# Layer norms on ScalarE, routing arithmetic on GpSimd, masked scores in PSUM and paired steps in a decoder-block kernel

## The chip, the cores and the metric

The kernel runs on one core of one Trainium2 chip. The metric is device time in microseconds, the median of several runs. The engines of a core have queues of their own, each worked off in order: TensorE (PE; its weight loads are shown as PEld), VectorE (DVE), ScalarE (ACT), GpSimd (POOL) and SyncE (SP), which here only issues DMAs. They wait for one another through semaphores.

## The reference

The input x has 4 x 1024 rows of 256 numbers, all float32. Three blocks follow one another, each added to x:

```python
x = x + attention(layernorm(x))       # 16 heads of 64, 4 key/value heads, no causal mask
x = x + cross(layernorm(x), context)  # 16 heads of 16, context of 64 rows, masked softmax
x = x + ffn(layernorm(x))             # routing, then a layer norm with gamma and beta
```

The ffn routes each row: scores against 8 cluster signatures go through a sigmoid and a table of 8 knots with linear interpolation (a calibration); the first largest picks a cluster. The scores of its 8 tiles go through the same calibration, and one tile is picked. A small network (gelu, tanh) gives two numbers per row; the picked tile's spline weights (two products, add, relu, dot product) turn them into one magnitude, which scales the picked tile's direction of 256 numbers. Direction plus input is normalised, times gamma, plus beta.

## The kernel before, in words

The 4096 rows are eight chunks of 512. Self-attention runs in 64 units (a chunk and a pair of heads) of 8 steps, one step for each 128 keys, 512 steps in all. In each step TensorE forms scores for a step (`scores`, L936), multiplies the exponentials of two steps ago with v (`attend`, L956) and forms the scores for a row maximum some steps ahead (`max_d` or `max_s`, L904). ScalarE takes the exponential (L1190) or, in every other step, a relu of the maximum scores too (L1174); VectorE reduces them to row maxima in the steps between (L1433) and adds up the first head's exponentials (L1449); GpSimd adds up the second head's (L1794). The maximum scores have a single pair of PSUM banks, `max_scores`, and so have the key scores.

Everything behind self-attention, for one chunk, is a `tail`: output projection (`out_proj`, `x1`), norm 1, cross-attention (`q2`, eight `scores2`/`soft2`/`exp2`/`weights2T`, `projected2`, `x2`), norm 2, `route`, `compress`, `gelu`, `comp`, two calibrations (`cal_a`, `cal_exp`, `cal_b`, `cal_c`) with `first_max`, `pick_tiles` and `pick_one`, `gathered`, `spline`, `y`, norm 3 with `gamma` and `beta`, `x3` and the store. The tail of a chunk is spread over the 64 attention steps of the next; the last chunk's is done at the end as two halves of 256 rows (`last_tail`), in alternation.

The order of all engines is one list that a planner, `Plan`, writes. A tail is a generator that stops at `yield EARLY` or `yield LATE`. In each step `attention` lets generators go on twice: the early pieces come ahead of TensorE's `attend`, the late ones behind it and ahead of the step's `scores` and maximum. So each `yield` moves what follows to the next such point, and every engine has a step's late pieces in its queue ahead of the step's exponential and row maximum. Pieces of TensorE take banks in turn from a ring of two, `misc` (2 and 6); units take them too (a projection of q, a transpose of maxima, the sums). `ALONE` is an early point at which no unit takes one. `BANK_FREE` names the signal that frees a bank, and how many counts before its end.

A norm is done so: VectorE takes `bn_stats` and `bn_aggr` (L1322, L1325), GpSimd adds epsilon and takes the power -0.5 (L1754, L1757), VectorE subtracts the mean and multiplies (`normalise`, L1329). Cross-attention's `soft2` adds the mask from PSUM into `weights` (L1545), takes the row maximum (L1549) and subtracts it (L1551). The other lines in the rows below: transposes of normed rows (L859), of picked tiles (L1091), the subtraction, products and sums of the knot arithmetic (L1615, L1627, L1630, L1632, L1634), `first_max` (L1641 and following), evictions of ScalarE with a bias (L1229) and without (L1251).

Of the kernel before, what the change touches and what calls it, by code (L numbers as in the profile page):

```python
# [13 lines left out]
P = 128  # L14
# [73 lines left out]
def unit(u):  # L88
# [9 lines left out]
    "x_stats": {"bn_stats": NT, "moments": NT, "var_eps": 1, "rstd": 1}, "x_norm": {"normed": NT},  # L98
# [15 lines left out]
    "out_proj": {"out_proj": 1}, "residual_bias": {"residual_bias": 1}, "x1": {"x1": 1},  # L114
    "stats": {"bn_stats": NT_TIMES, "moments": NT_TIMES, "var_eps": 1, "rstd": 1}, "norm": {"normed": NT_TIMES},
# [5 lines left out]
    "route": {"route": 1}, "route_ev": {"route_done": 1}, "compress": {"compressed": 1}, "gelu": {"gelu": 1},  # L121
    "comp": {"comp": 1}, "tanh_a": {"tanh": 2}, "tanh_exp": {"tanh_exp": 1}, "tanh_b": {"tanh": 3},
    "cal_a": {"gate": 1}, "cal_exp": {"gate_exp": 1}, "cal_b": {"gate": 6}, "cal_c": {"gate": 7},
    "first_max": {"pick": 5}, "pick_tiles": {"pick": 2}, "pick_one": {"pick": 1},
    "pickT": {"pickT": 1}, "pickT_ev": {"pickT_done": 1}, "gathered": {"gathered": 1},
    "gathered_ev": {"small": 1, "directions": 1}, "spline": {"spline": 8}, "y": {"y": NT_TIMES},
    "gamma": {"gamma": NT_TIMES}, "beta": {"beta": NT_TIMES}, "x3": {"x3": 1},
# [31 lines left out]
class Plan:  # L159
# [3 lines left out]
    def __init__(self):  # L163
        self.entries, self.seen = [], set()
        self.total, self.counts = {}, {}
        self.rings = {"max": [0], "key": [3], "misc": [2, 6]}
        self.turn = {name: -1 for name in self.rings}
        self.holder, self.banks = {}, {}

    def put(self, stage, *key):  # L170
# [3 lines left out]
        self.entries.append(entry)  # L174
        for name, times in signals_of(stage, key).items():
# [101 lines left out]
def calibration(plan, j, which):  # L277
# [6 lines left out]
    plan.put("cal_c", j, which)  # L284


def tail(plan, j):
# [3 lines left out]
    for i in range(nt):  # L291
# [5 lines left out]
        yield EARLY if i < nt - 1 else LATE  # L297
    plan.put("stats", j, 1)
    yield LATE
    plan.put("norm", j, 1)  # L300
    yield EARLY
    for c in range(KC):
        plan.put_in_bank("norm_T", j, 1, c)
        yield LATE
# [3 lines left out]
        yield EARLY  # L308
# [43 lines left out]
    for c in range(KC):  # L352
        plan.put_in_bank("norm_T", j, 2, c)
        yield LATE
        plan.put("norm_ev", j, 2, c)
        yield EARLY
    plan.put_in_bank("route", j)
    yield LATE
    plan.put("route_ev", j)
    yield EARLY  # L360
    plan.put_in_bank("compress", j)
    yield LATE
# [11 lines left out]
    plan.put("first_max", j, 0)  # L374
    plan.put("pick_tiles", j)
    yield LATE
    yield from calibration(plan, j, 1)
    plan.put("first_max", j, 1)
# [7 lines left out]
    for i in range(nt):  # L386
        plan.put_in_bank("gathered", j, i)
        yield LATE
        plan.put("gathered_ev", j, i)
        yield EARLY if i < nt - 1 else LATE  # L390
# [6 lines left out]
    yield LATE  # L397
    plan.put("beta", j)
    for pair in range(nt // 2):
        plan.put("x3", j, pair)  # L400
        if pair < nt // 2 - 1:
            yield LATE
# [141 lines left out]
class Workspace:  # L544


    def __init__(self, nt, first, allocate):
# [24 lines left out]
        self.hidden = flat[:, 3 * words:3 * words + 2 * nt * GRID].rearrange("p (a i n) -> p a i n", a=2, i=nt)  # L572
        self.mag = new("mag", nt)
# [3 lines left out]
        self.rstd = new("rstd", 2, nt)  # L577
# [15 lines left out]
def build(nc, ins, out):  # L593
# [5 lines left out]
    with ExitStack() as ctx:  # L599
# [13 lines left out]
        def before(signal, stage, *key):  # L613
            return plan.counts[(signal, stage, *key)][0]

# [141 lines left out]
        def rows_of(j):  # L757
            start = chunk_of(j) * CH + spaces[j].first * P
            return slice(start, start + tiles_of(j) * P)

# [87 lines left out]
        def _(tensor):  # L848
# [237 lines left out]
            def pickT(j):  # L1086
                ps = bank("pickT", j)
                pe.wait_ge(*freed("pickT", j))
                pe.wait_ge(*after("pick", "pick_one", j))
# [27 lines left out]
        def _(scalar):  # L1117
# [5 lines left out]
            def soft(k):  # L1123
                return main.c[:, :, :].rearrange("p a b -> p (a b)")[:, k * (HD + 1):(k + 1) * (HD + 1)]

# [85 lines left out]
            def norm_ev(j, k, c):  # L1211
# [5 lines left out]
                elif j < FIRST_HALF:  # L1217
                    act.wait_ge(*after("spline", "spline", j - 1))
# [4 lines left out]
            def q2_ev(j, m):  # L1223
# [3 lines left out]
                if 1 <= j < FIRST_HALF:  # L1227
                    act.wait_ge(*after("y", "y", j - 1))
# [25 lines left out]
            def route_ev(j):  # L1254
                nt, n = tiles_of(j), CL + TILES
                act.wait_ge(*after("route", "route", j))
                if 1 <= j < FIRST_HALF:
                    act.wait_ge(*after("pick", "pick_one", j - 1))
# [28 lines left out]
            def gathered_ev(j, i):  # L1287
                ps = bank("gathered", j, i)
                act.wait_ge(*after("gathered", "gathered", j, i))
                if 1 <= j < FIRST_HALF:  # L1290
                    act.wait_ge(*after("spline", "spline", j - 1))
# [615 lines left out]
```

## Time and profile before

| | us |
|---|---|
| median of 3 runs | 2048.97 (2048.21 to 2051.25) |
| the profiled execution's own time | 2041.75 |
| its span, first to last instruction | 2040.0 |
| TensorE busy | 1840.0 (90%) |
| VectorE busy | 1265.0 (62%) |
| ScalarE busy | 1135.5 (56%) |
| GpSimd busy | 912.8 (45%) |
| DMA queue 1, share of 16 engines | 5.4% |

The mean granted TensorE clock is 0.954 of full speed. A busy share says how long an engine worked, not whether the end depended on it; the waits and the timeline say that.

### The profile page before, as it was taken

Reading aid. Unit: us, or ns where it says so; the run is one execution under the profiler, and the core shown is the slowest. Engines: PE = TensorE matmul, PEld = TensorE weight load, DVE = VectorE, ACT = ScalarE, POOL = GpSimd, SP = SyncE. Lnnn points to the kernel's source line nnn. Section 1 sums busy time; section 2 is a strip of 40 time slices with the busy share of each in tenths; the row PEclk is TensorE's granted clock in tenths of the full one; section 3 lists DMA queues with packets and bytes.
Section 4 is the critical chain, followed back from the end, with each engine's and each line's share of the span. In section 5 each row is a group of like instructions: output and inputs, shape, how many; then the busy total and the mean of one; then the engine's idle time right before and its main releaser. Section 6 shows DMA issues by size and latency. Waiting matters only on the chain.

```text
span 2040.0 us, 27516 instructions
## 1 busy us (share of the span) xinstructions
PE 1840.0 (90%) x9556; PEld 904.5 (44%) x9556; DVE 1265.0 (62%) x2925; ACT 1135.5 (56%) x1507; POOL 912.8 (45%) x763
## 2 busy tenths in 40 slices
PE   2799999998999889998999989999899989999873
PEld 1554453453644444454454435345364434444341
DVE  4355646658476674756658665666747666475656
ACT  1266755765466654755557564565546655476422
POOL 2055445543554434552635433563454435354521
PEclk8799999998999999998999989999899999999986
DMA  5010000000200000010200000000010000000000
GB/s 151 1 45 19 1 1 1 11 22 1 62 11 1 0 1 21 1 32 1 61 3 11 1 1 21 1 11 21 2 51 1 1 1 22 1 1 1 21 1 10
DMA packets 22874, 32.01 MB, mean 16 GB/s; under 512 B 2576, under 2 KB 16976, under 8 KB 22736
## 3 DMA queue, kind: packets, MB, share of 16 engines
q1 hardware_dynamic: 22736, 30.26, 5.4%
q8 instruction: 75, 1.23, 0.3%
q14 instruction: 63, 0.52, 0.1%
HBM read 13.48 MB, written 4.19 MB: 9 GB/s over the span
## 4 chain that ended last, share of the span: by engine, by line
PE 73%; DVE 16%; issue 4%; ACT 4%; POOL 2%; DMA 1%; SPq 0%; POOLq 0%; DVEq 0%; ACTq 0%
PE attended L956 20%; PE key_scores L936 18%; PE misc L854 7%; PE max_scores L904 5%; PE misc L996 5%; PE misc L1020 3%; DVE relu L1433 2%; PE misc L966 2%; DVE running_sum L1449 2%; PE misc L922 2%; PE misc L1041 1%; PE misc L1052 1%; PE misc L1011 1%; PE misc L859 1%; ACT relu L1174 1%
## 5 line engine op out<-in xcount | busy, mean ns | idle before, releaser
L1190 ACT ACTIVATE probs<-key_scores 128x1024 f32<-128x1024 f32 x512 | 524.6, 1025 | 587.6 <-PE key_scores L936 435.6
L1794 POOL TENSOR_TENSOR prob_sum<-prob_sum,probs 128x512 f32<-128x512 f32 x384 | 507.1, 1321 | 247.7 <-ACT probs L1190 227.1
L956 PE MATMUL attended<-probs,v_all 128*64 128x512 f32 x2048 | 573.9, 634 | 0.7 <-ACT probs L1190 0.7
L1433 DVE CUSTOM_DVE_ANT_0 relu<-max_scores,relu 128x512 f32<-128x512 f32 x512 | 332.4, 686 | 310.1 <-PE max_scores L904 309.5
L936 PE MATMUL key_scores<-q_high,k_chain 64*128 64x512 f32 x2048 | 466.4, 451 | 9.5 <-ACT probs L1190 8.8
L936 PEld LDWEIGHTS key_scores<-q_high,k_chain 64*128 64x128 f32 x2048 | 195.6, 187 | 464.2 <-issue 250.9
L1174 ACT ACTIVATE relu<-max_scores 128x1024 f32<-128x1024 f32 x256 | 261.4, 1021 | 45.5 <-PE max_scores L904 45.5
L904 PE MATMUL max_scores<-k_max,q_high 64*128 64x512 f32 x1024 | 214.3, 414 | 67.9 <-DVE row_max L1433 66.3
L1790 POOL TENSOR_TENSOR prob_sum<-probs 128x512 f32<-128x512 f32 x64 | 86.7, 1354 | 360.9 <-PE misc L966 303.6
L1449 DVE TENSOR_TENSOR running_sum<-running_sum,probs 128x512 f32<-128x512 f32 x320 | 221.6, 692 | 16.1 <-ACT probs L1190 5.4
L936 PE MATMUL key_scores<-q_low,k_chain 64*128 64x512 f32 x1024 | 205.9, 398 | 0.0
L956 PEld LDWEIGHTS attended<-probs,v_all 128*64 128x64 f32 x2048 | 108.1, 137 | 184.8 <-issue 181.4
L1422 DVE SCALAR_TENSOR_TENSOR q_low<-misc,columns_sb,q_high 128x512 fp32r<-128x512 f32 x64 | 48.0, 750 | 170.1 <-ACT q_high L1165 169.7
L904 PEld LDWEIGHTS max_scores<-k_max,q_high 64*128 64x128 f32 x1024 | 99.5, 190 | 113.5 <-DVE row_max L1433 79.3
L1832 POOL TENSOR_TENSOR weights<-weights,row_stat 128x512 f32<-128x512 f32 x56 | 58.4, 1042 | 158.3 <-DVE row_stat L1561 152.9
L854 PE MATMUL misc<-xT,wq_hl 128*128 128x512 f32 x384 | 108.2, 418 | 0.0
L996 PE MATMUL misc<-wo,heads_out 128*128 128x256 f32 x448 | 103.5, 384 | 0.0
L1754 POOL TENSOR_SCALAR rstd<-moments 128x4 f32<-128x4 f32 x29 | 6.9, 238 | 210.3 <-DVE moments L1325 210.3
L936 PEld LDWEIGHTS key_scores<-q_low,k_chain 64*128 64x128 f32 x1024 | 99.4, 191 | 0.0
L996 PEld LDWEIGHTS misc<-wo,heads_out 128*128 128x128 f32 x448 | 82.8, 190 | 17.8 <-issue 7.3
L1803 POOL TENSOR_TENSOR heads_out<-raw_out,inv_sum 128x512 f32<-128x512 f32 x64 | 84.6, 1322 | 7.5 <-ACT inv_sum L1203 2.6
L854 PEld LDWEIGHTS misc<-xT,wq_hl 128*128 128x128 f32 x384 | 68.6, 191 | 34.7 <-issue 22.2
(420 smaller groups left out, 2198.9 us busy)
## 6 DMA issues: line engine op xcount, KB each, us to landing
k_chain<-k_chain SPq DMA_DIRECT2D x32, 256.0 KB, 3.8
buf_a<-in_x SPq DMA_DIRECT2D x8, 512.0 KB, 4.8
k_max<-k_max SPq DMA_DIRECT2D x16, 256.0 KB, 3.7
x_in<-in_x SPq DMA_DIRECT2D x7, 512.0 KB, 4.0
out_x<-buf_b SPq DMA_DIRECT2D x7, 512.0 KB, 3.2
heads_out<-in_qkv_wT SPq DMA_DIRECT2D x1, 1536.0 KB, 8.3
wo<-in_o_wT SPq DMA_DIRECT2D x1, 1024.0 KB, 13.0
rows_sb<-in_rows SPq DMA_DIRECT2D x1, 646.0 KB, 10.7
```

What stands on the lines that cost most here:

```text
L854: done = tensor.matmul(ps_out, lhs(a, c), rhs(b, c), start=n == 0, stop=n == len(terms) - 1)
L904: tensor.matmul(max_scores[:, head, :], q_high[u % 3][rows, i * P:(i + 1) * P], k_max[rows, place, g // 2, first:first + 512], start=True, ...
L936: done = tensor.matmul(key_scores[:, head, :], k_chain[rows, place, part, half, keys], q[rows, :], start=kt == 0 and part == 0 and q is hi ...
L956: tensor.matmul(attended[head * HD:(head + 1) * HD, :], v_all[:, kt, g * HD:(g + 1) * HD], prob_slot(u, kt, head), start=kt == 0, stop=kt ...
L996: done = tensor.matmul(ps[:, 0:D], heads_out[:, p, rows], wo[:, p, :], start=p == 0, stop=p == PAIRS - 1)
L1174: scalar.activation(relu[:, :, :], max_scores[:, :, :], ACT.Relu).then_inc(S["relu"])
L1190: scalar.activation(probs[(u * KT + kt) % len(probs)][:, :, :], key_scores[:, :, :], ACT.Exp).then_inc(S["exp"])
L1433: vector.tensor_tensor_reduce(out=relu[:, head, :], in0=max_scores[:, head, :], in1=relu[:, head, :], scale=1.0, scalar=-3.4e38, op0=ALU.a ...
L1449: vector.tensor_tensor(total, so_far, probabilities, ALU.add).then_inc(S["prob_sum0"])
L1790: gpsimd.tensor_tensor(prob_sum[1][:, :], prob_slot(u, 0, 1), probabilities, ALU.add).then_inc(S["prob_sum1"])
L1794: gpsimd.tensor_tensor(prob_sum[1][:, :], prob_sum[1][:, :], probabilities, ALU.add).then_inc(S["prob_sum1"])
L1803: gpsimd.tensor_tensor(heads_out[:, p, :], raw_out[:, :], inv_sum[:, :], ALU.mult).then_inc(S["heads_out"])
```

## The change

1. `normalise` moves from VectorE to ScalarE: an Identity activation with the reciprocal root as scale and minus mean times root as bias; GpSimd makes this bias with two more operations (`rstd` has four rows instead of two). The third norm is a norm of this kind too; then `gamma` is one product per pair of tiles on VectorE, `beta` is added to the residual rows on GpSimd at norm 2's place in the order, and `x3` adds both, pair by pair.
2. `bn_stats` follows each `x1`, `x2` and `y`; `stats` only aggregates. `y` goes by pairs.
3. `soft2` writes the masked scores back into their PSUM bank, takes the maximum there and subtracts from there into `weights`; the bank is free after that (`behind` 0 instead of 2).
4. `cal_c` is split. VectorE keeps `cal_b` (four operations), `cal_d` (a sum) and `cal_g` (two sums); GpSimd gets `cal_e` (four) and `cal_h` (two), `pick_tiles`, `pick_one` and the first four operations of `spline`; `mag` is the rest of the spline. Each has a step of its own.
5. In `tail`, a step without work follows the first norm too, both `norm_T` share a step, so do `route` and `compress`, and `gathered` goes by pairs.

```diff
-    "stats": {"bn_stats": NT_TIMES, "moments": NT_TIMES, "var_eps": 1, "rstd": 1}, "norm": {"normed": NT_TIMES},
+    "stats": {"moments": NT_TIMES, "var_eps": 2, "rstd": 2}, "norm": {"normed": NT_TIMES},
...
-    "norm_T": ("normT", "norm_ev", 0), "q2": ("q2_done", "q2_ev", 0), "scores2": ("soft2", "soft2", 2),
+    "norm_T": ("normT", "norm_ev", 0), "q2": ("q2_done", "q2_ev", 0), "scores2": ("soft2", "soft2", 0),
...
     plan.put("cal_b", j, which)
     yield LATE
-    plan.put("cal_c", j, which)
+    plan.put("cal_d", j, which)
+    plan.put("cal_e", j, which)
+    yield LATE
+    plan.put("cal_g", j, which)
+    plan.put("cal_h", j, which)
+    yield LATE
+    plan.put("first_max", j, which)
...
     plan.put("norm", j, 1)
+    yield LATE
     yield EARLY
     for c in range(KC):
         plan.put_in_bank("norm_T", j, 1, c)
-        yield LATE
+    yield LATE
+    for c in range(KC):
...
     plan.put_in_bank("route", j)
+    plan.put_in_bank("compress", j)
     yield LATE
     plan.put("route_ev", j)
-    yield EARLY
-    plan.put_in_bank("compress", j)
-    yield LATE
     plan.put("gelu", j)
...
-    for i in range(nt):
-        plan.put_in_bank("gathered", j, i)
+    for pair in range(nt // 2):
+        for i in range(2 * pair, 2 * pair + 2):
+            plan.put_in_bank("gathered", j, i)
         yield LATE
...
     plan.put("spline", j)
-    plan.put("y", j)
-    yield LATE
+    yield LATE
+    plan.put("mag", j)
+    for pair in range(nt // 2):
+        plan.put("y", j, pair)
+        yield LATE
     plan.put("stats", j, 3)
     yield LATE
-    plan.put("gamma", j)
-    yield LATE
-    plan.put("beta", j)
+    plan.put("norm", j, 3)
     for pair in range(nt // 2):
+        yield LATE
+        plan.put("gamma", j, pair)
         plan.put("x3", j, pair)
...
+            def normalise(space, src, dst):
+                for i in range(space.nt):
+                    scalar.activation(dst[:, i, :], src[:, i, :], ACT.Identity, bias=space.rstd[:, 3, i:i + 1],
+                                      scale=space.rstd[:, 1, i:i + 1]).then_inc(S["normed"])
...
+                scores3 = bank("scores2", j, n)[:, :].rearrange("p (h k) -> p h k", h=HB)
...
+                vector.tensor_tensor(scores3, scores3,
+                                     mask_add[:, b * SC:(b + 1) * SC].unsqueeze(1).broadcast_to([P, HB, SC]),
+                                     ALU.add).then_inc(S["soft2"])
+                dve.wait_ge(S["soft2"], base + 1)
+                vector.tensor_reduce(row_stat[:, 0, :], scores3, AX.X, ALU.max).then_inc(S["soft2"])
...
+            def cal_e(j, which):
+                space, n, base = spaces[j], tiles_of(j) * CL, before("knot", "cal_e", j, which)
+                gate, intervals = space.gate, space.intervals
+                pool.wait_ge(*after("gate", "cal_d", j, which))
+                gpsimd.tensor_tensor(intervals[:, :, 0:KNOTS - 1], intervals[:, :, 0:KNOTS - 1], intervals[:, :, 1:KNOTS],
+                                     ALU.subtract).then_inc(S["knot"])
...
```

## Rows read from the trace of the kernel before

**Rows 1.** The page, part 1: busy us and share of each engine.
```profile
PE 1840.0 (90%) x9556; PEld 904.5 (44%) x9556; DVE 1265.0 (62%) x2925; ACT 1135.5 (56%) x1507; POOL 912.8 (45%) x763
```

**Rows 2.** By stretch: us, PE, PEld, DVE, ACT, POOL busy; granted clock, DMA, GB/s.
```profile
0.00:100.00 100.00, 50.17 (x205) 34.11 (x206) 41.71 (x117) 21.15 (x29) 15.29 (x25) 0.76 0.26 77
...
100.00:1925.00 1825.00, 1725.82 (x9085) 833.07 (x9083) 1156.90 (x2607) 1084.09 (x1416) 866.21 (x705) 0.97 0.05 12
...
1925.00:2040.00 115.00, 64.05 (x270) 37.32 (x268) 66.35 (x202) 30.26 (x62) 31.32 (x34) 0.79 0.04 14
...
2000.00:2024.00 24.00, 7.61 (x24) 4.12 (x24) 20.16 (x97) 6.48 (x17) 0.00 (x0) 0.55 0.00 0
```

**Rows 3.** TensorE's waits, 100 to 1925 us: waiter <- awaited: us, times, longest.
```profile
PE max_scores L904 <- DVE row_max L1433: 57.2, 17, 7.1
...
PE misc L859 <- DVE buf_b L1329: 19.8, 6, 4.1
...
PE key_scores L936 <- ACT probs L1190: 8.8, 17, 1.5
...
PE misc L1091 <- DVE buf_c L1665: 6.0, 3, 2.9
...
PE misc L1041 <- POOL weights L1832: 4.9, 5, 1.0
```

**Rows 4.** Timeline, 458 to 464 us: start, duration, work [idle before <- awaited].
```profile
458.17 1.26 POOL L1794 TENSOR_TENSOR prob_sum<-prob_sum,probs 128x512 f32<-128x512 f32 x1
...
458.17 1.30 DVE L1634 TENSOR_TENSOR buf_c<-buf_c 128x32 f32<-128x32 f32 x1
...
459.51 0.19 DVE L1641 TENSOR_REDUCE mag<-buf_c 128x4 f32<-128x32 f32 x1
...
463.86 0.80 PE L904 MATMUL max_scores<-k_max,q_high 64*128 64x512 f32 x2 [5.48 <-DVE row_max L1433]
```

**Rows 5.** Timeline, norms at 14 and at 312 us.
```profile
14.41 2.08 DVE L1329 TENSOR_SCALAR buf_a<-buf_a,moments,rstd 128x256 f32<-128x256 f32 x4
...
311.71 4.36 DVE L1329 TENSOR_SCALAR buf_b<-buf_a,moments,rstd 128x256 f32<-128x256 f32 x4
...
316.12 1.12 PE L859 MATMUL misc<-consts_sb,buf_b 128*128 128x128 f32 x4 [4.12 <-DVE buf_b L1329]
```

**Rows 6.** VectorE lines: L1329 min/median/max ns; L1551 busy us, mean ns.
```profile
L1329 DVE TENSOR_SCALAR buf_b<-buf_a,moments,rstd x56: 399/1358/1443, 311.7 to 1855.8; 128x256 f32<-128x256 f32 x56
...
L1551 DVE TENSOR_TENSOR weights<-weights,row_stat 128x512 f32<-128x512 f32 x56 | 53.8, 960 | 1.9
...
L1551 DVE TENSOR_TENSOR probs<-probs,buf_c 128x512 f32<-128x512 f32 x2 | 1.4, 692 | 0.1
```

**Rows 7.** By stretch, 5 us behind two waits of TensorE.
```profile
315.00:320.00 5.00, 3.88 (x14) 1.86 (x16) 1.67 (x3) 0.60 (x1) 4.23 (x4) 0.66 0.02 3
465.00:470.00 5.00, 5.00 (x16) 1.45 (x12) 3.37 (x12) 2.66 (x4) 1.90 (x2) 0.53 0.00 2
```

**Rows 8.** Timeline, the loop's last long wait and one of the last tail's.
```profile
1890.41 0.79 PE L904 MATMUL max_scores<-k_max,q_high 64*128 64x512 f32 x2 [2.61 <-DVE row_max L1433]
...
2023.44 0.61 PE L1091 MATMUL misc<-consts_sb,p2T 128*64 128x128 f32 x2 [7.49 <-DVE p2T L1665]
```

**Rows 9.** Groups by form, GpSimd and VectorE: busy us, mean ns.
```profile
L1777 POOL TENSOR_TENSOR x_in<-x_in 128x384 f32<-128x384 f32 x8 | 8.0, 1005 | 0.6
...
L1775 POOL TENSOR_TENSOR x_in<-x_in 128x128 f32<-128x128 f32 x8 | 3.7, 458 | 0.6
...
L1627 DVE TENSOR_TENSOR buf_c<-buf_c,rows_sb 128x224 f32<-128x224 f32 x14 | 5.5, 392 | 0.5
...
L1757 POOL TENSOR_TENSOR rstd<-rstd,minus_half 128x4 f32<-128x4 f32 x29 | 30.2, 1041 | 2.4
```

**Rows 10.** Groups by form, ScalarE: 128x256 with a bias and without.
```profile
L1229 ACT ACTIVATE x_in<-misc,columns_sb 128x256 f32<-128x256 f32 x1 | 0.5, 464 | 0.0
...
L1251 ACT ACTIVATE buf_d<-misc 128x256 f32<-128x256 f32 x28 | 10.7, 382 | 3.9 <-PE misc L1030 3.9
```

More of the change, by code:

```diff
@@ L296, in tail @@
         plan.put("x1", j, i)
[L297 removed]
+        if i < nt - 1:
+            yield EARLY
     plan.put("stats", j, 1)
@@ new lines, in cal_d, with cal_g @@
+            def cal_d(j, which):
+                dve.wait_ge(*after("gate", "cal_b", j, which))
+                vector.tensor_reduce(gates_flat(j, 1), spaces[j].intervals[:, :, 1:KNOTS], AX.X, ALU.add).then_inc(S["gate"])
+            def cal_g(j, which):
+                dve.wait_ge(*after("knot", "cal_e", j, which))
+                vector.tensor_reduce(gates_flat(j, 1), picked_knots(j), AX.X, ALU.add).then_inc(S["gate"])
+                vector.tensor_reduce(gates_flat(j, 2), spaces[j].steps_by[:, :, 0:KNOTS - 1], AX.X, ALU.add).then_inc(S["gate"])
@@ L1695, in y @@
+            def y(j, pair):
+                space, tiles = spaces[j], range(2 * pair, 2 * pair + 2)
+                dve.wait_ge(*after("mag", "mag", j))
                 dve.wait_ge(*after("directions", "gathered_ev", j, space.nt - 1))
-                for i in range(space.nt):
+                dve.wait_ge(*after("normed", "norm", j, 2))
+                for i in tiles:
                     vector.scalar_tensor_tensor(
@@ L1709, in beta_ @@
-            def beta_(j):
-                space = spaces[j]
-                dve.wait_ge(*after("rstd", "stats", j, 3))
-                dve.wait_ge(*after("gamma", "gamma", j))
-                for i in range(space.nt):
-                    vector.scalar_tensor_tensor(
-                        out=space.b[:, i, :], in0=space.b[:, i, :], scalar=space.rstd[:, 1, i:i + 1], in1=beta[:, :],
-                        op0=ALU.mult, op1=ALU.add).then_inc(S["beta"])
+                dve.wait_ge(*after("y", "y", j, pair))
@@ L1725, in _ @@
-                "spline": spline, "y": y, "gamma": gamma_, "beta": beta_,
+                "cal_b": cal_b, "cal_d": cal_d, "cal_g": cal_g, "first_max": first_max,
+                "tile_scores": tile_scores, "mag": mag_, "y": y, "gamma": gamma_,
             }
@@ new lines, in cal_h, with pick_tiles @@
+            def cal_h(j, which):
+                gate, base = spaces[j].gate, before("knot", "cal_h", j, which)
+                pool.wait_ge(*after("gate", "cal_g", j, which))
+                gpsimd.tensor_tensor(gate[:, 0], gate[:, 0], gate[:, 2], ALU.mult).then_inc(S["knot"])
+                pool.wait_ge(S["knot"], base + 1)
+                gpsimd.tensor_tensor(gate[:, 6 if which else 3], gate[:, 0], gate[:, 1], ALU.add).then_inc(S["knot"])
+            def pick_tiles(j):
+                tiles = spaces[j].route[:, :, CL:].rearrange("p i (c t) -> p i c t", c=CL)
+                pool.wait_ge(*after("pick", "first_max", j, 0))
+                gpsimd.tensor_tensor(spaces[j].picked_by[:, :, :, :], tiles,
+                                     spaces[j].gate[:, 4].unsqueeze(3).broadcast_to([P, tiles_of(j), CL, TPC]),
+                                     ALU.mult).then_inc(S["picked"])
```

275 lines of the change are left out of this document (138 added, 137 removed), and 2 rows, old and new, of the table SIGNALS.

## The prediction

> **What bounds the kernel now.** I read the busy shares first. TensorE is busy 1840.0 of 2040.0 us, VectorE 62%, ScalarE 56%, GpSimd 45% [rows 1]: TensorE sets the end, so a change elsewhere pays only where TensorE stands still or runs at a lower clock. The table by stretch splits the 200 us of idleness: 50 in the first 100 us, 99 in the 1825 us of the attention loop, 51 in the last 115 us [rows 2]. The table of TensorE's waits then says who is late in the loop: 57.2 us in 17 waits for VectorE's row maxima, 19.8 in 6 for the layer norm written by VectorE, 8.8 for the exponentials, 6.0 for the picked tiles, 4.9 for the cross weights [rows 3]. Those five make 96.7 of the 99.
>
> The timeline shows the mechanism twice. At 458.2 VectorE is inside the knot arithmetic of a tail. A 128x32 operation of that piece takes 1.30 us while GpSimd adds into its running sum, against 0.19 for a neighbour; the row maxima stand behind them in VectorE's queue, `max_scores` is not free, and TensorE waits 5.48 us [rows 4]. At 311.7 the four norm instructions take 4.36 us instead of the 1.6 that 0.4 us each, the fastest, would make; the transposes wait 4.12 us [rows 5, 6]. The median of 1.36 us over 56 such instructions shows that this is the rule in the loop.
>
> The idle time is not all of the loss. In the 5 us after the wait at 463.86 the granted clock is 0.53 with TensorE busy all the time, and it is 0.66 after the one at 316.12 [rows 7], where the engine had just stood still for 4 to 5 us; 1.0 and 0.53 mark the two levels of 2.4 and 1.2 GHz. That costs 5 x 0.47 = 2.4 and 5 x 0.34 = 1.7 us more, 2 us on average. The loop has 17 waits of at least 2.4 us, the first at 316.12 and the last at 1890.41 [rows 5, 8]: some 34 us. So norms and routing hold 99 + 34 = 133 us in the loop at most.
>
> **Part 1: routing.** Now `cal_c` (7 operations), `first_max` (5) and `pick_tiles` (2) share a step, 14 dependent operations ahead of one row maximum, and `cal_b` puts 6 there in another. Afterwards a step holds at most five small ones: four in `cal_b`, one in `cal_d`, two in `cal_g`, five in `first_max`; and the two-input ones that GpSimd held up go to GpSimd. `first_max` keeps three of that kind. Five at 0.19 to 0.4 us are 1 to 1.5 us. I let 85% of 57.2 + 6.0 go: **-54**. What is late next is GpSimd: VectorE's `cal_g` waits for `cal_e`, four operations. From 458 ns at 128 columns and 1005 at 384 [rows 9] a line gives 0.66 us at 224 and 0.25 at 32, so `cal_e` is 2.3 us against about 1.4 on VectorE (0.39 each, rows_sb form, [rows 9]). It stands behind one running sum of 1.3 us on GpSimd [rows 4]; a step lasts about 3 us, so it is done mostly when asked for. Fourteen calibrations with two such waits at 0 to 2 us each: 0 to 56 us; I take 0.2 each, near the cover, **+5**. The `spline`, `pick` and `beta` pieces on GpSimd are read a step later and lie beside attention; without that cover they would cost their own 1 us per tail.
>
> **Part 2: norms on ScalarE.** The 19.8 us go, and with them the part of the 8.8 us and of the maxima that the slow norm and gamma passes cause (about 4.5): **-24**. ScalarE has to do the norm in its place, ahead of the next exponential in its queue. A 128x256 activation with a bias takes 0.46 us, without one 0.38 [rows 10]; a second per-partition operand should add the same 0.08, so four are some 1.9 to 2.1 us. The Trainium skill (ScalarE: Activation LUTs, What ACT_TABLE_LOAD costs) says that every such pointer operand adds about 93 ns; the bias row agrees, the scale has no row. TensorE has about 0.3 us of slack behind an exponential, but steps with projections have 1 to 2. 27 norms in the loop (7 tails x 3, 6 input blocks), each 0 to 1.8 us: 0 to 49; I take 0.6, because the free step puts the reciprocal root on GpSimd (1.04 us for the power and two more operations of about 0.25, by the line above) behind it: **+16**. Before that step `norm` is queued one step behind `stats`; if GpSimd is late, ScalarE waits and the exponential and relu behind it, then TensorE. That is inside the upper bound.
>
> **Part 3: the two banks.** Pairs of transposes, `route` with `compress`, and pairs of `gathered` now take both banks of the ring in one step. Where a q projection, a transpose of maxima or the sums take one in the same step, TensorE waits for an eviction by ScalarE (0.38 us and more [rows 10]) that stands behind other work. Counting the steps of all seven tails gives 9 such steps. Each costs between 0 (freed in time) and 3 us; I take 1.2: **+11**. The tail's length stays: in the schedule the calibrations add 4 steps, the end 2, the norms take 3 off and the gathers 2, beside 60 to 64 steps now, of 64 that a block of rows has. A tail that runs over makes the next start late, and only the last would show, by a step of 3 us.
>
> **Part 4: scores in PSUM.** The bank is released after the subtraction, 1.4 us later. In two steps of each tail another user is near: 14 times 0 to 1 us; **+3**. The subtraction reads PSUM and one small operand: now 960 ns on average against 692 where GpSimd rests [rows 6], so 56 x 0.27 = 15 us of VectorE go, all hidden; that only makes the 85% likelier.
>
> **Clock.** Of the 34 us, three or four long waits should stay: **-26**.
>
> **The two ends.** At the start the second norm (2.08 us [rows 5]) leaves VectorE, whose chain leads to the key projection; the first is 0.7 us later through two more GpSimd operations: -1. At the end VectorE is busy 20.16 of 24 us with two serial halves [rows 2]; half of that goes to GpSimd, with handovers, and one wait of 7.49 [rows 8] gets shorter: -4. The norms there have no cover: two per half plus the last, 0.6 us more each, and the final scaling about +1: +4. Together **-1**, between -8 and +8.
>
> **Sum**, against the profiled execution's 2041.75 us: -54 + 5 - 24 + 16 + 11 + 3 - 26 - 1 = -70, so 1972. The median of the runs is 7.2 us above the profiled one, so **1979 us** (-3.4%). A run of this kernel tells about 0.2%, 4 us, from no change.
>
> **Rivals.**
> *A, given back inside the loop* (0.15): the exponentials become the wait. 27 norms at 1.5 us (41) and 9 bank steps at 2.5 (23) plus 14 us of GpSimd waits, and waits above 2.4 us keep half of the clock loss (-17): -54 - 24 + 41 + 23 + 14 + 3 - 17 - 1 = -15: 2034. For it: ScalarE is 56% busy and TensorE already waits 17 times on it [rows 3]; against: these waits are 0.5 us on average, and activations of this length occur in each unit without one.
>
> *B, slower, the port and queue of GpSimd* (0.10): the moved arithmetic is at least 1.7 times as long there, and each of its two-input operations holds VectorE's (1.30 for 0.19 [rows 4]). The row maxima then stand behind VectorE waiting for `cal_e`, `pick_tiles` and `cal_h`. Price: if two of GpSimd's 1.3 us operations and `cal_e` line up (4.9 us, less 1.5 of cover), 28 waits of 3.4 us are 95, and the clock loss stays: -54 + 95 - 24 + 16 + 11 + 3 - 1 = +46: 2095. It decides from 1.8 us per wait on, where the sum passes zero (95 - 46 = 49 us over 28). The Trainium skill (GPSIMD Engine Reference, Engine selection) says elementwise work belongs on VectorE, GpSimd being about half as fast with two inputs. The skill (SBUF, Who interferes with whom) calls the pair of ports an exclusive lock against VectorE operations with two SBUF inputs. The rows agree with the lock. By these rules the move would be a loss, were TensorE not waiting on the queue's order rather than on VectorE's sum.
>
> *C, the steps matter and not the engines* (0.02, no change): waits reappear one step on, under other names: within 4 us.
>
> *Forecast* 0.73. Its own range is 1950 to 2012 (norms 0.2 to 1.3, bank steps 0.5 to 2, 70 to 95% of the waits gone). With A inside, 8 times in 10: **1942 to 2032**. Chances: faster 0.73 + 0.15 = 0.88; same 0.02; slower 0.10.
>
> **What would show it.** TensorE's waits on the row maxima under 12 us in the loop, those on the norm in `buf_b` under 3; a busy TensorE near 1810 with a granted clock of 0.98 or more in the loop; waits on the exponentials up from 8.8 to 15 to 30, at norm steps; a few waits at the second transpose, at `compress` and at the second `gathered`. VectorE's busy time down by about 150, GpSimd's up by 80 to 90, ScalarE's by 45 to 60. The forecast is wrong if waits on `cal_e`'s results stand in front of the row maxima, if the waits on exponentials exceed 40 us, or if the clock stays at 0.97.

## The result, and the profile after

The changed kernel takes 2029.93 us (median of 4 runs, 2027.29 to 2033.37) against 2048.59 for the kernel before beside it: ratio 0.9909, interval 0.9889 to 0.993. That is 0.9% faster where 3.4% was forecast. Single runs differ by some us: the profiled one of before was 7 us under its median, the one of after (2033.37) is 3 over, so the two traces differ by only 8.4 us. The result lies inside the stated range by 2 us, and outside the forecast's own range of 1950 to 2012.

First the busy shares of the changed kernel, as in [rows 1].

```profile
PE 1838.3 (90%) x9556; PEld 909.0 (45%) x9556; DVE 1150.5 (57%) x2619; ACT 1196.9 (59%) x1635; POOL 1007.9 (50%) x1011
```

Then its table by stretch, as in [rows 2].

```profile
0.00:100.00 100.00, 50.57 (x208) 34.47 (x208) 39.27 (x110) 25.48 (x38) 15.96 (x29) 0.78 0.26 78
100.00:1925.00 1825.00, 1733.17 (x9138) 840.69 (x9137) 1062.80 (x2364) 1139.96 (x1530) 956.25 (x907) 0.98 0.05 13
1925.00:2032.00 107.00, 54.57 (x214) 33.80 (x212) 48.44 (x147) 31.45 (x68) 35.73 (x75) 0.70 0.02 5
```

And TensorE's waits between 100 and 1925 us, as in [rows 3].

```profile
PE key_scores L961 <- ACT probs L1236: 37.3, 38, 3.6
PE max_scores L929 <- DVE row_max L1473: 27.9, 19, 4.4
PE misc L947 <- DVE weights L1584: 7.1, 10, 0.7
PE misc L879 <- DVE weights L1584: 3.8, 8, 0.5
PE misc L1125 <- ACT shift_row L1226: 2.9, 3, 1.0
PE misc L884 <- DVE q_low L1462: 2.8, 4, 1.2
PE misc L1066 <- POOL weights L1829: 2.6, 4, 0.6
PE misc L1116 <- POOL buf_c L1866: 2.3, 2, 1.2
PE misc L1066 <- DVE weights L1584: 2.2, 3, 0.9
```

VectorE lost 114.5 us and TensorE stands still almost as long as before: all rows of this view make 89.4 us against 98.4. The row maxima fell from 57.2 to 27.9, the norm's 19.8 are gone, and in their place stand 37.3 us on exponentials and 13.1 on banks that `soft2` (L1584) still reads. From the first to the last `attend` the loop is 13.4 us shorter (1837.07, now 1823.70), it starts 0.7 us earlier, and what follows it is 5.7 us longer.

Most of these 5.7 us lie behind the last matmul (1.4 ahead of it). GpSimd adds the first half's result there and only then begins the second half's spline; VectorE waits for that:

```profile
2018.67 1.26 POOL L1805 TENSOR_TENSOR weights<-weights 128x512 f32<-128x512 f32 x1 [1.99 <-DVE weights L1706]
2020.01 0.24 POOL L1876 TENSOR_TENSOR p2T<-probs 128x32 f32<-128x32 f32 x1
...
2021.25 0.19 DVE L1681 SCALAR_TENSOR_TENSOR p2T<-p2T,probs 128x32 f32<-128x32 f32 x1 [2.72 <-POOL p2T L1882]
```

From its statistics to its last addition the second half then takes 4.8 us (2024.1 to 2028.9) where it took 3.6 (2033.7 to 2037.3): the root's two more operations, the activation and the product stand in series.

Three places show what is late now. ScalarE at the second norm of the tail that runs beside a batch's last chunk, GpSimd's queue ahead of it, and TensorE behind it (timelines):

```profile
407.55 1.01 POOL L1774 TENSOR_TENSOR x_in<-x_in 128x384 f32<-128x384 f32 x1
408.64 0.23 POOL L1746 TENSOR_SCALAR rstd<-moments 128x4 f32<-128x4 f32 x1
...
410.38 0.20 POOL L1754 TENSOR_TENSOR rstd<-rstd 128x4 f32<-128x4 f32 x1
...
410.62 2.08 ACT L1153 ACTIVATE buf_b<-buf_a,rstd 128x256 f32<-128x256 f32 x4 [1.34 <-POOL rstd L1754]
412.60 1.00 ACT L1236 ACTIVATE probs<-key_scores 128x1024 f32<-128x1024 f32 x1
...
413.65 0.50 PE L961 MATMUL key_scores<-q_high,k_chain 64*128 64x512 f32 x2 [3.60 <-ACT probs L1236]
```

The root's four GpSimd operations begin only after the key projection's differences (L1774), ScalarE idles 1.34 us for them, the norm takes 2.08, and the exponential starts at 412.60. The change's free step does not help here: it lies behind the norm, ahead of the transposes, and between statistics and norm there is one step as before. Waits of 3.60 and 3.63 us recur at 892.75 and 1373.02. ScalarE's waits for the root in the same 1825 us:

```profile
ACT buf_b L1153 <- POOL rstd L1754: 11.7, 13, 2.3
ACT x_in L1153 <- POOL rstd L1754: 4.6, 4, 1.7
```

So the root was late at 17 of the 27 norms, by 16.3 us in all.

VectorE in `first_max` (L1662 to L1670), then the row maximum (L1473) and TensorE:

```profile
447.67 0.19 DVE L1662 TENSOR_REDUCE mag<-buf_c 128x4 f32<-128x32 f32 x1 [0.74 <-POOL buf_c L1854]
447.89 1.14 DVE L1664 TENSOR_TENSOR buf_c<-buf_c,mag 128x32 f32<-128x32 f32 x1
449.07 1.31 DVE L1666 TENSOR_TENSOR buf_c<-buf_c,consts_sb 128x32 f32<-128x32 f32 x1
...
452.15 0.79 PE L929 MATMUL max_scores<-k_max,q_high 64*128 64x512 f32 x2 [2.52 <-DVE row_max L1473]
```

VectorE where `mag` (L1688) and both pairs of `y` (L1696, each with two `bn_stats`, L1367) stand between two row maxima:

```profile
732.01 1.33 DVE L1688 TENSOR_SCALAR mag<-mag,rows_sb 128x4 f32<-128x4 f32 x1
733.38 0.88 DVE L1696 SCALAR_TENSOR_TENSOR buf_b<-buf_d,mag,buf_b 128x256 f32<-128x256 f32 x2
734.29 0.75 DVE L1367 BATCH_NORM_STATS2 stats<-buf_b 128x6 f32<-128x256 f32 x2
...
735.55 0.87 DVE L1696 SCALAR_TENSOR_TENSOR buf_b<-buf_d,mag,buf_b 128x256 f32<-128x256 f32 x2
736.46 0.75 DVE L1367 BATCH_NORM_STATS2 stats<-buf_b 128x6 f32<-128x256 f32 x2
...
738.48 0.72 PE L929 MATMUL max_scores<-k_max,q_high 64*128 64x512 f32 x2 [4.45 <-DVE row_max L1473]
```

The granted clock in the 5 us behind the last two of these waits, as in [rows 7]:

```profile
452.15:457.15 5.00, 5.00 (x16) 2.09 (x16) 3.79 (x8) 1.48 (x3) 2.06 (x2) 0.50 0.00 0
738.48:743.48 5.00, 5.00 (x20) 2.09 (x22) 1.46 (x7) 3.66 (x7) 3.62 (x6) 0.66 0.00 0
```

TensorE was busy all the time, at 1.2 GHz for all (0.50) or much (0.66) of it. I take "clock loss" below as TensorE's busy time times one minus the granted clock, added up over the 365 stretches of 5 us of the loop: 35.6 us before, 26.1 after. Waits of 2.4 us or more went from 17 (69.0 us) to 8 (27.2 us).

### The profile page after: what moved, and what is told of

The parts are those of the page before. It is cut to its first block and busy times, and to the rows that moved or that the text cites. A ratio compares the mean times of both kernels' runs of the same rounds, so it can differ in the third digit from the quotient of the medians.

```text
span 2031.6 us, 27706 instructions
## 1 busy us (share of the span) xinstructions
PE 1838.3 (90%) x9556; PEld 909.0 (45%) x9556; DVE 1150.5 (57%) x2619; ACT 1196.9 (59%) x1635; POOL 1007.9 (50%) x1011
## 5 line engine op out<-in xcount | busy, mean ns | idle before, releaser
L981 PE MATMUL attended<-probs,v_all 128*64 128x512 f32 x2048 | 566.2, 626 | 0.1
L1473 DVE CUSTOM_DVE_ANT_0 relu<-max_scores,relu 128x512 f32<-128x512 f32 x512 | 333.0, 688 | 382.1 <-PE max_scores L929 381.0
L961 PE MATMUL key_scores<-q_high,k_chain 64*128 64x512 f32 x2048 | 464.7, 450 | 38.4 <-ACT probs L1236 37.3
L879 PE MATMUL misc<-xT,wq_hl 128*128 128x512 f32 x384 | 107.8, 416 | 3.9 <-DVE weights L1584 3.8
L1489 DVE TENSOR_TENSOR running_sum<-probs 128x512 f32<-128x512 f32 x64 | 94.5, 1476 | 0.7 <-ACT probs L1236 0.7
L879 PEld LDWEIGHTS misc<-xT,wq_hl 128*128 128x128 f32 x384 | 68.5, 191 | 39.3 <-issue 18.5
## 6 DMA issues: line engine op xcount, KB each, us to landing
wo<-in_o_wT SPq DMA_DIRECT2D x1, 1024.0 KB, 13.1
rows_sb<-in_rows SPq DMA_DIRECT2D x1, 646.0 KB, 10.8
```

Source lines behind the costliest of these rows:

```text
L879: done = tensor.matmul(ps_out, lhs(a, c), rhs(b, c), start=n == 0, stop=n == len(terms) - 1)
L961: done = tensor.matmul(key_scores[:, head, :], k_chain[rows, place, part, half, keys], q[rows, :], start=kt == 0 and part == 0 and q is hi ...
L981: tensor.matmul(attended[head * HD:(head + 1) * HD, :], v_all[:, kt, g * HD:(g + 1) * HD], prob_slot(u, kt, head), start=kt == 0, stop=kt ...
L1473: vector.tensor_tensor_reduce(out=relu[:, head, :], in0=max_scores[:, head, :], in1=relu[:, head, :], scale=1.0, scalar=-3.4e38, op0=ALU.a ...
L1489: vector.tensor_tensor(total, so_far, probabilities, ALU.add).then_inc(S["prob_sum0"])
```

## The experiments

The changed kernel once more:

> The changed kernel itself, unaltered, beside the others on one chip. Both theories: 0.991 of the kernel before, within 0.002 (2030 us on a chip where the kernel before takes 2048.6).

0.9916 (0.9891 to 0.994). All ratios are to the kernel before, run in turn on the same chip. "Waits" are TensorE's between 100 and 1925 us of the profiled run; where a kernel is faster, this stretch takes in a little of what follows the loop.

### Which part brought what

**Norms back on VectorE.**

```diff
-scalar.activation(dst[:, i, :], src[:, i, :], ACT.Identity, bias=space.rstd[:, 3, i:i + 1], scale=...)
+vector.tensor_scalar(dst[:, i, :], src[:, i, :], space.moments[:, i, 0:1],
+                     space.rstd[:, 1, i:i + 1], ALU.subtract, ALU.mult)
```

> The changed kernel (2030 us, 0.9909 of the kernel before) with one thing put back: all norms are VectorE's tensor_scalar with mean and reciprocal root again, at the same places in the order, and everything else as changed. Theory 1 (the ScalarE norms gave the gain back): four activations of 2.08 us stand ahead of an exponential, and they make most of the rise of TensorE's waits on exponentials from 8.8 to 37.3 us. With the norms gone from ScalarE these waits fall under 18, the waits on the norm itself stay under 8 (the first norm has a free step behind it now), row-maximum waits rise by 5 to 12 us from 27.9; time 2015 to 2026. Rival (moving the norms was worth it, as I forecast, net -8 us): row maxima and norm waits rise by 30 us or more, time 2036 or more. A rise of the exponential waits that does not come from the norms would leave them above 30.

1.0008 (0.9991 to 1.0026). Waits of this kernel:

```profile
PE max_scores L929 <- DVE row_max L1473: 47.3, 26, 4.6
PE misc L884 <- DVE buf_b L1369: 13.5, 3, 4.5
PE key_scores L961 <- ACT probs L1215: 10.1, 27, 1.1
```

The exponentials do fall by 27.2 us, but row maxima and norm bring 32.9 back, and clock loss rises from 26.1 to 36.9. Theory 1 is wrong: in this kernel the norms on ScalarE are worth 1.0%, although they made the exponentials the largest wait.

**Cross scores in `weights` again** (`"scores2": ("soft2", "soft2", 2)` and the old `soft2`).

> The changed kernel with the cross scores handled as before: the mask is added from PSUM into weights and the bank is free after that one operation. Theory: the 13 us in which TensorE waits for a misc bank that soft2 still reads (transposes of maxima, q projections, cross scores; 0.3 to 0.7 us each, 20 odd times) go, and VectorE's 15 us more are hidden; time 2016 to 2024. Rival: the longer VectorE operations (two SBUF inputs, held up by GpSimd) push row maxima and cross weights later by as much; time 2027 or more, with waits on row maxima up from 27.9 to 38 or more.

0.9875 (0.985 to 0.99), 0.3% under the changed kernel, with intervals that overlap a little. The trace is clearer: no wait on `weights` L1584 is left for a bank, row maxima stay at 27.9, and TensorE's idle time between the first and the last `attend` falls by 8.7 us. It is not the whole 13.1, because the waits on the cross weights rise from 2.6 to 6.9. So keeping the scores in PSUM cost some 0.3%, at the edge of what these runs tell.

**Routing arithmetic back on VectorE, same steps** (`cal_e`, `cal_h`, `pick_tiles`, `pick_one`, `spline` as VectorE stages).

> The changed kernel with its steps, but the arithmetic that went to GpSimd (cal_e, cal_h, pick_tiles, pick_one, the first four operations of the spline) done by VectorE in the same steps. Theory: what took the routing stalls down from 57.2 to 27.9 us was the splitting into steps, not the engine; a step has at most five to six small operations either way. The waits on row maxima stay at 28 to 36 us, time 2028 to 2038. Rival (the engine matters, the two-input operations are held up by GpSimd's own adds, 1.3 instead of 0.2 us each): waits on row maxima above 45 us, time 2045 or more. Third reading (GpSimd's added work costs through the port and its queue): time 2024 or less.

1.0047 (1.0028 to 1.0067): 1.4% slower than the changed kernel. Row-maximum waits 40.3 instead of 27.9, waits for picked tiles 5.3 instead of 2.3. I had expected no difference. The engine matters, though the row maxima stayed under the 45 us that the rival named. GpSimd is no faster at the work. Here is one of the four operations of `cal_e`, on GpSimd in the changed kernel and on VectorE in this one (mean of 14):

```profile
L1839 POOL TENSOR_TENSOR buf_c<-buf_c,rows_sb 128x224 f32<-128x224 f32 x14 | 8.9, 638 | 1.1
L1715 DVE TENSOR_TENSOR buf_c<-buf_c,rows_sb 128x224 f32<-128x224 f32 x14 | 13.7, 975 | 0.5
```

The means of all four add up to 2.18 us on GpSimd and to 2.19 on VectorE.

**Only the order, then order and GpSimd.** `a_steps_only` puts back all three parts, `a_route_only` leaves the arithmetic on GpSimd. "The order" here includes the third norm's new form (gamma and beta apart, beta on GpSimd), the spread `bn_stats` and the root's two more operations.

> The changed kernel with three of its parts put back at once: norms on VectorE, the routing arithmetic on VectorE, cross scores in weights. What is left of the change is its order: split calibration steps, two-bank steps, bn_stats spread out, y by pairs, the free step and the third norm in its new form. Theory (parts add up): 0.9909 + 0.0099 for the norms + 0.0138 for the arithmetic - 0.0034 for the scores = 1.011, so 2066 to 2078 us on a chip where the kernel before takes 2048: the new order by itself is slower than before, and the engines pay for it. Rival C of my prediction (the steps bring the gain, engines do not matter): 0.995 or less. Third reading (the two moves off VectorE overlap, either relieves the same row maxima): 1.003 or less.

> The changed kernel with norms on VectorE and cross scores in weights again, so of the change only the order and the routing arithmetic on GpSimd are left (parts 1 and 3 of my prediction, to which it gave -54 + 5 + 11 of waits and most of the clock's 26 us, 0.97 of the kernel before). Theory now (splitting shortens single waits but makes more of them, GpSimd's part just pays for the order): row-maximum waits 44 to 52 us against 57.2 before, 0.995 to 1.000. Rival (the parts disturb each other, each alone is better): 0.990 or less.

1.0065 (1.0041 to 1.0089), between the sum of the parts (1.011) and the reading that they overlap (1.003), and 0.9946 (0.9926 to 0.9966). The row maxima of the first and of the second kernel:

```profile
PE max_scores L929 <- DVE row_max L1473: 66.8, 29, 4.6
```
```profile
PE max_scores L929 <- DVE row_max L1473: 49.5, 26, 4.6
```

The new order by itself raises 17 waits of 57.2 us [rows 3] to 29 of 66.8. Ahead of the row maximum at 445 us of the first kernel, `cal_e` on VectorE alone takes 3.4 us for four operations, two of them stretched, and leaves a wait of 3.82. Together the kernels make a chain: before 1; order 1.0065; arithmetic on GpSimd 0.9946; norms on ScalarE 0.9875; scores in PSUM 0.991.

**Norms on ScalarE in the kernel before**: those of the input blocks and norms 1 and 2. The third, with gamma and beta, stays as it was.

> The kernel before with one part of the change: the norms of the input blocks and norms 1 and 2 are ScalarE activations, the bias made by two more GpSimd operations; order, routing, cross scores and the final scaling as before. Theory (the effect seen in the changed kernel is one of the part itself): the 19.8 us of waits on the norm go, waits on exponentials rise from 8.8 to 25 to 35 us, four waits above 4 us become some of 2 to 3.6; 0.992 to 0.998 (my prediction's sum for the part: -24 + 16 and some 7 of clock). Rival (it is worth as much as in the changed kernel, 0.990): 0.991 or less.

1.0015 (1.0 to 1.003): no gain. Waits of this kernel:

```profile
PE max_scores L908 <- DVE row_max L1450: 61.5, 19, 7.1
PE key_scores L940 <- ACT probs L1215: 14.6, 21, 2.2
PE misc L863 <- ACT buf_b L1132: 9.0, 4, 2.3
```

Nearly half of the norm's wait stays, since TensorE now waits for a 2 us norm on ScalarE that itself waits 0.8 us for the root. Both theories missed. Nearly the same edit (20 of the loop's 27 norms) is worth 1.0% in one surrounding and nothing in another.

### Length, lateness or place

**Norms in two steps of two tiles**, and **a free step more ahead of whole norms**. Both give each tail the same length, its pieces the same steps.

```diff
-    plan.put("norm", j, 1)
-    yield LATE
+    for pair in range(nt // 2):
+        plan.put("norm", j, 1, pair)
+        yield LATE
```
```diff
     plan.put("stats", j, 1)
     yield LATE
+    yield LATE
     plan.put("norm", j, 1)
```

Norms 2 and 3 and those of the input blocks are changed alike.

> The changed kernel with each four-tile norm on ScalarE put in two steps of two activations (1.04 us each instead of 2.08), so a tail is up to 5 steps longer and still ends within its 64. Theory: TensorE's 19 odd waits of 1.8 to 3.6 us behind a norm shrink to under 1 us each; waits on exponentials fall from 37.3 to 12 to 20 us, the granted clock of the loop rises from 0.98 by up to 0.01; time 2002 to 2016. Rival (the waits are a rhythm of the exponential queue and come back at another step): waits on exponentials stay above 28, time 2025 or more.

> The changed kernel with one more free step between the statistics and each norm, the norms in one piece of four activations. Each tail and each piece of it falls at the same step as in the kernel with the norms in halves (0.9783), so the two differ in the length of ScalarE's block alone. Theory L (length: 2.08 us in one block): only the part of the 3.6 us waits that comes from a late reciprocal root goes (1.3 us, three times), waits on exponentials 28 to 34 us, 0.988 to 0.992. Rival S (it was the shift: the norm later and the pieces at luckier steps): waits on exponentials fall to about 17 us as in halves, 0.981 or less.

0.9783 (0.9756 to 0.981) and 0.9827 (0.9802 to 0.9852). Their waits on exponentials, halves first:

```profile
PE key_scores L966 <- ACT probs L1241: 16.6, 37, 2.8
```
```profile
PE key_scores L966 <- ACT probs L1241: 18.7, 30, 1.3
```

Both are far below 37.3. Clock loss is 8.8 and 14.6 us. Of the 1.3% against the changed kernel, 0.8 came with the extra step alone, with norms of 2.08 us as before; the other 0.4 lies within overlapping intervals. Rival S was nearer than my theory of length. With the step ahead of the norm, this is all that ScalarE still waits for the root, where it was 16.3 us:

```profile
ACT buf_b L1158 <- POOL rstd L1759: 0.6, 1, 0.6
```

In halves it still waits 10.0 us in 8 norms. So the two kernels do not differ in length alone, as I had written, and the shorter block may be worth more than 0.4%. The extra step also does two things at once: it gives the root time and it moves every later piece. No run parts the two.

**A stop between `mag` and `y`** (`yield LATE` behind `plan.put("mag", j)`).

> The changed kernel with one step more: a stop between mag and the first pair of y, so the four mag operations no longer share a step with two y and two bn_stats. Theory: the two waits of 4.4 us on row maxima behind y (at 738 and 1218 us) fall under 1.5 us each, and the clock after them is kept; row-maximum waits from 27.9 to about 22 us, time 2017 to 2024, 5 to 11 us less than the changed kernel. Rival (two y and two bn_stats alone, 3.2 us, are too long for a step anyway): the waits stay above 3 us, time within 3 us of the changed kernel.

0.9935 (0.9917 to 0.9952) beside 0.9916 for the changed kernel: nothing gained. The waits of 4.4 us became 3.3 and 3.4, row maxima in all rose to 31.3. The rival was right: both pairs of `y` still stand between two row maxima.

**The tail moved as a whole**: `FINISH_BEHIND + 1` becomes `+ 2` or `+ 3`, nothing else.

> The changed kernel with each tail of the loop begun one attention step later; nothing else altered. Theory P (placement is a cause of its own: each piece now meets another kind of step, since row maxima fall in every other one): the time moves by 8 us or more either way, ratio outside 0.9875 to 0.995, and the table of waits changes its rows. Rival Q (parts alone count): 0.991 within 0.003.

> The changed kernel with each tail begun two steps later, so pieces meet the same kind of step (row maximum or relu) as in the changed kernel but other projections and sums. Theory P1 (what matters is which piece stands ahead of a row maximum): 0.991 within 0.003. Theory P2 (projections of q, k, v and the norms of input blocks beside the pieces matter too): outside of that, with the three waits of 3.6 us on exponentials beside the key projection gone or moved.

> The kernel before with each tail begun one step later; nothing else altered. Theory P: ratio outside 0.996 to 1.004, because the 14 operations of the knot arithmetic then stand in another kind of step. Rival Q: 1.000 within 0.003.

> The kernel before with each tail begun two steps later; nothing else altered. Theory (two steps cost the changed kernel 1.0% and the effect belongs to the placement, whatever the parts): 1.008 to 1.02, so that the change is worth 0.7 to 2% there too. Rival (the effect is one of the changed kernel's own pieces): 1.000 within 0.004, and the change is worth nothing at this placement.

| tail begins | before | changed | changed / before |
|---|---|---|---|
| as is | 1 | 0.9909 (0.9889 to 0.993) | 0.991 |
| 1 step later | 1.0154 (1.0126 to 1.0182) | 0.9875 (0.9854 to 0.9897) | 0.973 |
| 2 steps later | 1.0102 (1.0077 to 1.0127) | 1.0013 (0.9998 to 1.0029) | 0.991 |

The last column is the quotient; its interval is 0.002 to 0.004 to either side. A shift that changes no instruction moves the time by up to 1.5%, more than the whole change. The kernel before, one step later, at the norm and at the row maxima:

```profile
PE max_scores L904 <- DVE row_max L1433: 59.0, 18, 7.1
PE misc L859 <- DVE buf_b L1329: 30.7, 9, 5.0
```

and two steps later, with one of its norms:

```profile
PE max_scores L904 <- DVE row_max L1433: 82.9, 32, 5.5
```
```profile
675.51 5.50 DVE L1329 TENSOR_SCALAR buf_b<-buf_a,moments,rstd 128x256 f32<-128x256 f32 x4 [0.95 <-POOL rstd L1757]
```

So the kernel before stood at the best of its three places. Theory P holds for `b_shift1`; `a_shift1` (0.9875) ended on P's limit. P1 is refuted: two steps on, pieces meet the same kind of step and the time still moves 1%.

### Combinations

`best1` has norms in halves, scores in `weights` and the stop behind `mag`; `best3` is without the stop; `best2` is `best1` without the free step behind norms 1 and 2 and with one between the pairs of `y`; `best1_shift1` begins its tails a step later.

> The changed kernel with three edits together: each norm in two steps of two tiles, cross scores handled as before, a stop between mag and y. Theory (each removes its own waits and the clock loss behind them): 0.9783 (norms in halves) - 0.0034 - 0.005, so 0.970, 1980 to 1992 us on a chip where the kernel before takes 2048; waits in the loop under 62 us against 87, granted clock in the loop 0.99. Rival (one wait covers for another, so that the last ones removed bring little): 0.977 or more, 2000 us or more.

> The changed kernel with the norms in halves and the cross scores handled as before, without the stop between mag and y that the first combined kernel (0.9722) has. Theory (the stop is worth nothing, as it was in the changed kernel alone): 0.970 to 0.975. Rival (the stop takes the waits of 4.4 us down to 2.2 and their clock loss with them): 0.977 or more.

> The first combined kernel (0.9722) with the free step behind norms 1 and 2 taken out and one put between the two pairs of y. Theory: a row maximum then has one pair of y (2 x 0.87 + 2 x 0.38 us) ahead of it instead of two; the waits of 2.2 to 3.4 us on row maxima behind y go; waits in the loop from 60 to 50 to 56 us; 0.965 to 0.970. Rival (steps of the tail shift, and other pieces meet the row maxima): within 0.002 of 0.9722.

> The first combined kernel (0.9722) with each tail begun one step later; three tails then end on or past their 64 steps and two start a step late. Theory (shorter pieces make the kernel less sensitive to placement): 0.972 within 0.005. Rival (as sensitive as the others): outside of that, and a lower value would be the best kernel.

0.9722 (0.9702 to 0.9742), 0.975 (0.9727 to 0.9774), 0.9814 (0.9788 to 0.9839) and 0.9756 (0.973 to 0.9782). `best1` is the fastest kernel here, 1989.23 us where before takes 2044.96: 1.9% under the changed one. Its waits:

```profile
PE max_scores L935 <- DVE row_max L1479: 35.2, 28, 3.4
PE key_scores L967 <- ACT probs L1242: 11.6, 28, 1.0
```

`best2` missed its forecast. Its row maxima did fall, to 24.9 us, but without the free step the exponentials rose from 11.6 to 25.8, and what follows the last `attend` grew by 7.1 us:

```profile
PE key_scores L967 <- ACT probs L1242: 25.8, 35, 2.7
```

The stop behind `mag`, worthless alone, may be worth 0.3% here (intervals overlap). One step later the best kernel is 0.3% slower, with intervals that overlap. That does not show it to be less sensitive to its place: the first step moved the changed kernel by no more, and a second step was not tried.

## Why the prediction was wrong in size

The direction and the wide range held; the point estimate was 51 us off. That the range held is luck in part: it was widened towards rival A, and the result lies 2 us inside that end. Of the three signs of being wrong that were written down, two did not appear (waits on exponentials are 37.3 where over 40 was the sign, the clock is 0.98) and waits on `cal_e` were small (6.7 us of VectorE's), while the row maxima stood at 27.9 where under 12 was said. The traces against the terms of the sum (us):

| term | forecast | trace |
|---|---|---|
| routing stalls (row maxima and picked tiles, 63.2) | -54 | -33.0 (to 30.2) |
| norm waits and their share of others | -24 | -19.8 |
| ScalarE norms ahead of exponentials | +16 | +28.5 |
| steps with three banks | +11 | +6.2 (L1125, L884, L1097) |
| scores in PSUM | +3 | +10.8 (13.1 on banks, -2.3 on cross weights, 4.9 to 2.6) |
| GpSimd handovers | +5 | none of TensorE's by itself; VectorE waits 6.7 us, in 7 waits, for `cal_e` |
| clock | -26 | -9.5 |
| two ends | -1 | +5.0 |

The trace's column makes -11.8. With the 1.7 us that waited on the sums before and do not now, it is -13.5, against -8.4 between the profiled runs; the loop's own part of this gap, 5 us, stays unexplained.

**Routing, the step that failed.** "Five at 0.19 to 0.4 us are 1 to 1.5 us. I let 85% of 57.2 + 6.0 go." The five of `first_max` took 3.0 us at 448 us: two of them (1.14, 1.31) were held by GpSimd's running sum, the very row [rows 4] that I had read, and I costed them at their undisturbed length. Of the 33 us only some 12 are the routing's own: with order and GpSimd alone (`a_route_only`) row maxima and picked tiles still make 51.3 us (49.5 and 1.8) of the 63.2, and the rest left only with the norms (30.2 in `a_soft2_sbuf`). I also put all 57.2 us on the knot arithmetic. The kernel before waits 2.8 us at 499.23 behind `spline` and `y`, and the new step of `mag`, two `y` and two `bn_stats`, which my sum never costed, leaves 4.45 us. And a wait is what exceeds the slack between two row maxima; cut into three, a long piece can exceed it three times. The order alone gave 29 waits for 17.

**Who removed what.** Rival C gave the steps everything; the runs say the reverse. Order +0.65%, GpSimd -1.2%, ScalarE -0.7% (-1.0% with the scores in PSUM). Rival B, that GpSimd's port and queue would make the routing slower, is refuted by `a_route_vector`. The rule of the Trainium skill (GPSIMD Engine Reference, Engine selection) cited for it would have kept the arithmetic on VectorE, which costs 1.4% here. I also expected `cal_e` to take 2.3 us on GpSimd and 1.4 on VectorE. It takes 2.18 and 2.19, as VectorE's operations are stretched beside GpSimd's sums. So the move gave up no time and took the work off the queue that TensorE waits on.

**Norms.** "I take 0.6, because the free step puts the reciprocal root on GpSimd [...] behind it." It was 28.5/27 = 1.06 us each. The free step covers nothing of the root: it stands behind the norm. The root was late at 17 of 27 norms, and at three of them, beside a key projection, TensorE waited 3.6. A step ahead of the norm brought these waits of ScalarE from 16.3 to 0.6 us and the exponentials from 37.3 to 18.7. The duration was right: four activations take 2.08 us (1.9 to 2.1 forecast). Rival A named this mechanism with 1.5 us a norm and its 2034 is nearest to the result; but taking it away (`a_norm_vector`) did not pay, so it was a price and not the cause of the loss. The norm's gain also came partly through the row maxima, as no norm stands ahead of them on VectorE (47.3 to 27.9).

**Scores in PSUM.** "14 times 0 to 1 us" was 21 waits of 13.1 us: the bank is held by three operations of 0.69 us, and transposes of maxima (L947) and q projections (L879) come more often than the two steps of each tail that I counted.

**Clock.** The pool was right (34 forecast, 35.6 read). I kept three or four long waits; eight of 2.4 us or more stayed and norms leave some of 1.8 to 2.1 us, behind which the clock is lower too (0.66 in the 5 us from 976). In the norm kernels a clock loss of 8.8 and 14.6 us goes with 7 and 5 long waits in the same 1825 us, against 8 and 26.1 in the changed one. So the count of long waits does not tell the loss by itself.

**What no term held.** The place of the tail. My sum took each piece's wait from before and let it shrink. Each new step moves all later pieces to other projections and row maxima, and a shift of the whole tail was worth up to 1.5% by itself. At one step later the change is worth 2.7%, nearer to the forecast of 3.4; as delivered 0.9. So the share of each part above holds for this placement, and how much of it is placement is open; only averages over several shifts could say.

**The ends.** I let the end gain 4 us by shared work and lose 4 by handovers, so that both ends together came to -1. It lost 5.7: with no attention beside it, each handover of the final chain is in the time. From the last `attend` to the end the traces show 113.5 us in the changed kernel, 110.2 with the arithmetic on VectorE, 111.4 with the norms there, 108.3 with all three parts back and 107.9 before. So the arithmetic on GpSimd makes some 3.3 us of the loss and the norms on ScalarE some 2.2, by one trace each. VectorE for the last tail's arithmetic alone was not tried.

## What to carry to other kernels

Where several in-order queues feed one bound engine, cost a piece by what stands between it and the next operation that the bound engine awaits, at its disturbed duration, and list every piece of the step, not only those that the edit names. Taking work off the queue that is awaited can pay even where the other engine is no faster at it; splitting it in place may not. Ask on which side of a piece a free step lies, and what it covers there. Before a change of one per cent is put down to its content, shift the schedule by a step or two in both kernels: here that alone moved the time by 1.5%, and a step added ahead of the norms brought 0.8%, about as much as the norms on ScalarE.

## What the hardware showed that I had not expected

A 128x4 `tensor_scalar` with one SBUF tensor and a pointer scalar (`mag`, L1688) took 1.33 us under GpSimd's running sum and 0.23 in the last tail, where its form is 128x2 and GpSimd rests; the same 128x4 operation took 0.23 on average in the kernel before. Four norms of at least 0.4 us each took 5.50 at 675.51. So not only operations with two tensors from SBUF are held. The Trainium skill (SBUF — State Buffer, Who interferes with whom) lists `tensor_scalar` among those that can take the shared pair in a two-port mode, when their operands meet its conditions. Whether these do, no row tells. VectorE's operations of `soft2` on PSUM were never stretched: all three kinds take 0.69 us in the changed kernel (0.67 to 0.70), where the subtraction took 0.96 on average before [rows 6].
